# Cross-attention's last step: weight splits, norms, token halves and statistics put behind the chain of the last quarter

## The reference

```python
x = layernorm(x + self_attention(x))                 # 32 heads of 16, causal
x = layernorm(x + cross_attention(x, ctx, ctx, mask))  # 32 query heads of 128, 8 key/value heads
x = layernorm(x + moe(x))                            # top 4 of 16 experts, and a shared expert

# cross_attention
q, k, v = x @ wq, ctx @ wk, ctx @ wv                 # wq 512x4096, wk and wv 512x1024
q, k = rope(q), rope(k)
w = softmax(where(mask, q @ k.T / sqrt(128), -1e9))  # a group of 4 query heads shares a key head
out = (w @ v) @ wo                                   # wo 4096x512
```

## Time and profile before

| | |
|---|---|
| median of three runs | 1835.05 us |
| profiled execution | 1827.3 us, its span 1825.5 us |
| busy share of the span | TensorE 94%, VectorE 73%, ScalarE 50%, GpSimd 49% |
| end of the cross-attention block | 1324.2 us after the span's start |
| what comes after it | routing and shared expert, then 79 expert tiles, then the last layer norm |

### The profile page before, as it was taken

One profiled execution on the slowest core, in us unless ns is written; L12 is line 12 of the kernel. 1 busy time (PEld: TensorE's weight loads), 2 busy tenths in 40 slices (PEclk: granted clock), 3 DMA queues, 4 the chain that ended last, 5 costly groups with the idle time before them and its releaser, 6 DMA issues. The chain is left out here.

```text
span 1825.5 us, 39028 instructions
## 1 busy us (share of the span) xinstructions
PE 1717.9 (94%) x15412; PEld 992.6 (54%) x15412; DVE 1337.6 (73%) x2260; ACT 917.5 (50%) x1532; POOL 894.6 (49%) x732
## 2 busy tenths in 40 slices
PE   6999999899999999999999999999798999999990
PEld 4767666455555555555555555555454555455550
DVE  5788788688888888888888888887788444344445
ACT  4565656655546555555555554646531333233334
POOL 6643022554646555555546464646342555455540
PEclk9999999999999999999999999999899999999995
DMA  9620010211413213223222131212135678887658
GB/s 250 170 47 21 8 61 3 93 65 41 139 58 100 85 61 112 69 73 113 70 70 93 36 123 40 93 47 71 64 123 176 151 151 219 208 215 152 118 97 288
DMA packets 84947, 190.41 MB, mean 104 GB/s; under 512 B 10849, under 2 KB 29665, under 8 KB 82721
## 3 DMA queue, kind: packets, MB, share of 16 engines
q1 hardware_dynamic: 61680, 129.55, 21.0%
q0 software_dynamic: 23088, 58.37, 15.7%
HBM read 124.68 MB, written 63.21 MB: 103 GB/s over the span
## 5 line engine op out<-in xcount | busy, mean ns | idle before, releaser
L288 PE MATMUL bank<-xhl,front_h 128*128 128x512 f16 x704 | 267.8, 380 | 15.0 <-DVEq L68 13.4
L289 PE MATMUL bank<-xhl,front_h 128*128 128x512 f16 x704 | 267.6, 380 | 0.0
L290 PE MATMUL bank<-xhl,front_l 128*128 128x512 f16 x704 | 267.6, 380 | 0.0
L1000 POOL TENSOR_TENSOR xa_xs<-xa_xs,sn 128x512 f32<-128x512 f32 x160 | 233.7, 1460 | 45.8 <-ACT xa_xs L1047 45.8
L1011 POOL TENSOR_TENSOR xa_sc<-xa_sc,xa_rs 128x1024 f32<-128x1024 f32 x32 | 62.2, 1945 | 382.3 <-DVE xa_rs L1241 382.3
L1005 POOL TENSOR_TENSOR xa_rr<-xa_x,xa_xs 128x512 f32<-128x512 f32 x160 | 231.7, 1448 | 12.7 <-DVE xa_x L1147 0.2
L288 PE MATMUL bank<-out_h,xa_oh 128*128 128x512 f16 x512 | 194.1, 379 | 9.3 <-DVE xa_ol L1132 6.6
L1880 POOL DMA_INDIRECT scratch_y<-raw_front,moe_to x79 | 125.2, 1585 | 150.3 <-DVE mo_zl L1933 112.6
L290 PE MATMUL bank<-out_h,xa_ol 128*128 128x512 f16 x512 | 194.0, 379 | 0.0
L289 PE MATMUL bank<-out_l,xa_oh 128*128 128x512 f16 x512 | 194.0, 379 | 0.0
L1046 ACT ACTIVATE xa_xs<-bank 64x512 f32<-64x512 f32 x160 | 94.9, 593 | 131.7 <-PE bank L290 128.0
(11 more groups left out here) (292 smaller groups left out, 4758.1 us busy)
## 6 DMA issues: line engine op xcount, KB each, us to landing
xa_rawc<-in_ew SPq DMA_DIRECT2D x32, 768.0 KB, 5.6
moe_ring<-scratch_w SPq DMA_DIRECT2D x16, 1536.0 KB, 8.7
scratch_w<-xa_chunk_h SPq DMA_DIRECT2D x32, 384.0 KB, 2.3
scratch_w<-xa_chunk_l SPq DMA_DIRECT2D x32, 384.0 KB, 3.3
raw_front<-in_xwq SPq DMA_DIRECT2D x8, 1024.0 KB, 7.8
raw_out<-in_xwo SPq DMA_DIRECT2D x8, 1024.0 KB, 5.3
scratch_y<-xa_zero SPq DMA_DIRECT2D x18, 256.0 KB, 6.0
acc<-in_x POOLq DMA_DIRECT2D x4, 1024.0 KB, 12.8
```

The source lines that it names most:

```text
L288: pe.matmul(out_ap, ah, bh, start=start and m == 0, stop=False)
L289: pe.matmul(out_ap, ah, bl, start=False, stop=False)
L290: mm = pe.matmul(out_ap, al, bh, start=False, stop=stop and m == n - 1)
L1000: PO.mark(pool.tensor_tensor(xr, xr, sn[:, :].rearrange("p (a s) -> p a s", a=1) .to_broadcast([P, QT // S, S]), ALU.mult), f"sm{r}", st)
```

## The change

Everything stands in the last step (7, 3) and the tail. In the step, the high half of the last weight chunk is no longer made behind the exponentials, nor its low half at the step's end. The low half of the shared expert's weights is no longer made between `w0` and `w1`. Of the low token halves of quarter 0, two stay where they were and two move behind the reciprocal. In the tail, the statistics of quarter 2 move from first place on VectorE to behind the `back_lo` splits; the chunk's high half follows `back_p` on ScalarE, its low half follows the statistics and the aggregation on VectorE, and the shared expert's low half stands between the inverse and the adds of `w1` to `w3`. Two semaphores replace the events for the last chunk; the events' counts are kept by naming them with others.

```diff
@@ SyncE, in the loop over steps
-                            sp.wait_ge(DV.sem, DV.value("cl", Step(i, q)))
-                            met(sp)
+                            if (i, q) == (NG - 1, NQ - 1):
+                                sp.wait_ge(s_last_l, 1)
+                            else:
+                                sp.wait_ge(DV.sem, DV.value("cl", Step(i, q)))
+                                met(sp)
                             store_chunk(i, q)
@@ ScalarE, step
+                    def chunk_hi(i, q):
+                        act.wait_ge(s_cr, i * (16 * NQ) + 16 * (q + 1))
+                        act.wait_ge(s_cw, i * (32 * NQ) + 32 * (q + 1))
+                        return act.activation(chunk_h[:, :], rawc[:, :], ACT.Copy, scale=WS)
...
-                        act.wait_ge(s_cr, i * (16 * NQ) + 16 * (q + 1))
-                        act.wait_ge(s_cw, i * (32 * NQ) + 32 * (q + 1))
-                        AC.mark(act.activation(chunk_h[:, :], rawc[:, :], ACT.Copy, scale=WS), "ch", st)
+                        if (i, q) != (NG - 1, NQ - 1):
+                            AC.mark(chunk_hi(i, q), "ch", st)
@@ ScalarE, tail
                     back_p(Step(None, 0))
+                    chunk_hi(NG - 1, NQ - 1).then_inc(s_last_h, 1)
                     back_o(Step(None, 0), range(4))
@@ VectorE, step
-                            back_add(st, [0])
-                        if q == 3:
+                            back_add(st, [0], ("wfl",) if (i, q) == (NG - 1, NQ - 1) else ())
+                        if q == 3 and i < NG - 1:
                             dve.wait_ge(AC.sem, AC.value("wfh", st))
                             DV.mark(split_front_lo(dve, i), "wfl", st)
...
-                        if i == NG - 1 and q == 3:
-                            for t in range(TQ):
+                        last = (i, q) == (NG - 1, NQ - 1)
+                        if last:
+                            for t in range(2):
                                 after.low(dve, 0, t, bank[4 + t])
...
                         DV.mark(dve.reciprocal(rs[:, :, :], sm[:, :, :]), "rc", st, ("w3",) if alone else ())
+                        if last:
+                            for t in range(2, TQ):
+                                after.low(dve, 0, t, bank[4 + t])
                         if not alone:
-                            back_add(st, [3])
-                        dve.wait_ge(AC.sem, AC.value("ch", st))
-                        DV.mark(dve.scalar_tensor_tensor(chunk_l[:, :], ...), "cl", st)
+                            back_add(st, [3], ("cl",) if last else ())
+                        if not last:
+                            dve.wait_ge(AC.sem, AC.value("ch", st))
+                            DV.mark(chunk_lo(), "cl", st)
@@ VectorE, tail
-                    dve.wait_ge(DV.sem, DV.value("w3", st, 1))
-                    after.statistics(dve, 2, range(TQ))
                     back_p_lo(st)
                     for t in range(TQ):
                         after.low(dve, 1, t, bank[(2, 3, 0, 1)[t]])
+                    back_lo(st, range(4))
+                    dve.wait_ge(DV.sem, DV.value("w3", st, 1))
+                    after.statistics(dve, 2, range(TQ))
                     after.aggregate(dve, 2)
-                    back_lo(st, range(4))
+                    dve.wait_ge(s_last_h, 1)
+                    chunk_lo().then_inc(s_last_l, 1)
                     dve.wait_ge(s_gate, 16)
...
                     back_add(st, [0])
                     after.inverse(dve, 2, 1)
+                    dve.wait_ge(AC.sem, AC.value("wfh", Step(NG - 1, NQ - 1)))
+                    split_front_lo(dve, NG - 1)
                     back_add(st, [1, 2, 3])
```

More of the change, by code:

```diff
@@ L864, in cross_attention @@
                 s_cr, s_cw, s_xr = sem("xa_s_cr"), sem("xa_s_cw"), sem("xa_s_xr")
+                s_last_h, s_last_l = sem("xa_last_h"), sem("xa_last_l")
                 zero, s_zero, s_zeros = b("zero", [P, D]), sem("xa_zero"), sem("xa_zeros")
@@ L1098, in step @@
                             s2 = sc[:, h, :, :, :].rearrange("p a b c -> p (a b c)")
-                            AC.mark(act.activation(s2, s2, ACT.Exp, scale=float(HD2) ** -0.5), f"ex{h}", st)
-                        act.wait_ge(s_cr, i * (16 * NQ) + 16 * (q + 1))
-                        act.wait_ge(s_cw, i * (32 * NQ) + 32 * (q + 1))
-                        AC.mark(act.activation(chunk_h[:, :], rawc[:, :], ACT.Copy, scale=WS), "ch", st)
+                            AC.mark(act.activation(s2, s2, ACT.Exp, scale=float(HD2) ** -0.5), f"ex{h}", st,
+                                    ("ch",) if (i, q, h) == (NG - 1, NQ - 1, 1) else ())
+                        if (i, q) != (NG - 1, NQ - 1):
+                            AC.mark(chunk_hi(i, q), "ch", st)
                         if i == NG - 1 and q >= 2:
@@ L1133, in back_lo, with chunk_lo, back_add @@
                                                       heads(oh, tp, b2), ALU.subtract), f"lo{c}", st)
-                    def back_add(st, ts=range(TQ)):
+                    def chunk_lo():
+                        return dve.scalar_tensor_tensor(chunk_l[:, :], rawc[:, :], WS, chunk_h[:, :], ALU.mult, ALU.subtract)
+                    def back_add(st, ts=range(TQ), also=()):
                         for t in ts:
@@ L1139, in back_add @@
                             DV.mark(dve.scalar_tensor_tensor(row, home[f"w{t}"][:, :], 1 / (WS * OS), row,
-                                                             ALU.mult, ALU.add), f"w{t}", st)
+                                                             ALU.mult, ALU.add), f"w{t}", st, also)
                     def cosine(st, r, also=()):
@@ L1241, in step @@
                         DV.mark(dve.reciprocal(rs[:, :, :], sm[:, :, :]), "rc", st, ("w3",) if alone else ())
+                        if last:
+                            for t in range(2, TQ):
+                                after.low(dve, 0, t, bank[4 + t])
                         if not alone:
-                            back_add(st, [3])
-                        dve.wait_ge(AC.sem, AC.value("ch", st))
-                        DV.mark(dve.scalar_tensor_tensor(chunk_l[:, :], rawc[:, :], WS, chunk_h[:, :], ALU.mult, ALU.subtract), "cl", st)
+                            back_add(st, [3], ("cl",) if last else ())
+                        if not last:
+                            dve.wait_ge(AC.sem, AC.value("ch", st))
+                            DV.mark(chunk_lo(), "cl", st)
                     for i in range(NG):
@@ L2133, in build @@
             ln2 = NormSteps("ln2", numbered("st", 0) + ["ag0", "iv0", "sh0"] + numbered("st", 1) + ["ag1", "iv1", "sh1"] + numbered("lo", 0)
-                            + numbered("st", 2) + numbered("lo", 1) + ["ag2", "iv2", "sh2"] + numbered("st", 3) + ["ag3", "lo2.0", "iv3", "sh3"]
+                            + numbered("lo", 1) + numbered("st", 2) + ["ag2", "iv2", "sh2"] + numbered("st", 3) + ["ag3", "lo2.0", "iv3", "sh3"]
                             + numbered("lo", 2, (1, 2, 3)) + numbered("lo", 3),
```

## The result

The changed kernel takes 1833.93 us (median of 20 runs, 1830.23 to 1838.46), the kernel before 1828.87 us (median of 20, 1825.58 to 1836.12). The ratio is 1.0027, 95% interval 1.0018 to 1.0036: 3.3 to 6.6 us slower, a quarter of a per cent. TensorE reached the tail's output matmuls 8 us sooner, and yet the barrier behind them came 5.4 us later.

The account below looks back on a forecast made before the run. TensorE was taken to set the barrier at 1324.2 us, SyncE 0.9 behind; the chunk's 6.9 us delay through SyncE's chain puts it at 1330.1, +5.9 us: 1833.2 profiled, 1841 on the median, 1838 taken; range 1828 to 1845.

Parts of the forecast that it names:

- the two levels of three runs: Runs before: one at 1825.58 us, two near 1835.5; the new median was put between the levels, at 1838.
- The gain ahead of it: Last step and tail's front: reciprocal ready at 1294.9 us, output matmuls starting at 1304 instead of 1311.62, 7.6 us earlier.
- The chunk's low half: VectorE's tail: the last chunk's low half, taking 3.13 us, ends at 1311.0 instead of 1304.09, 6.9 us later.
- SyncE's chain: Chunk store, quarter 0 rows, GpSimd's quarter 1 pass, second store: 18.9 us without slack, all moved on by 6.9 us.
- The new idle of 3.4 us: TensorE's tail output matmuls: wait for VectorE's add of w0 to free bank 0 before w2, 3.4 us.
- Behind the barrier: Next block, entered with TensorE idle for 7 to 10 us: 0 cost, 1.5 us as upper bound.
- the idle start: TensorE enters the block behind the barrier from idle instead of full clock; taken as 0, at most 1.5 us.
- Rival 1: At the barrier: TensorE sets the end after all, 0.9 to 3.5 us earlier, 1823.8 to 1826.4 us profiled; 10%.
- Rival 2: Shared expert's matmuls behind the barrier: TensorE stays at 1.2 GHz, +22 us with the shift, 1849 us profiled; 4%.
- Rival 3: At the barrier: little of the chunk's 6.9 us delay arrives, 0 to +4 us, 1827 to 1831 us profiled; 12%.

Follow-up runs that it names:

- experiment 1: The changed kernel with SyncE storing both sets of token rows ahead of the last weight chunk; ratio 0.9971 to the kernel before.
- experiment 3: The changed kernel with only the last chunk's split put back into the step; ratio 0.9977 to the kernel before.
- experiment 4: The changed kernel with the last chunk's low half moved to the very end of VectorE's tail; ratio 1.0075 to the kernel before.
- experiment 5: The kernel before with only the last chunk's high and low halves moved as in the change; ratio 1.0051 to the kernel before.
- experiment 2: The kernel before with both sets of token rows stored ahead of the last weight chunk; ratio 1.0013 to the kernel before.
- experiment 6: The changed kernel with 52 unused matmuls added at the end of TensorE's tail; ratio 1.0030 to the kernel before.
- experiment 7: As experiment 1, with the adds of w0 and w1 moved earlier in VectorE's tail, w0's ahead of the chunk's low half; ratio 0.9953 to the kernel before.

## Why the prediction was right

The forecast was +5.9 us against the profiled execution of before, through one mechanism: the last chunk's store comes later, the rows stand behind it in SyncE's queue, GpSimd behind the rows, their store behind GpSimd. Measured were +5.4 us to the barrier and +5.1 us between the medians. Experiments 1, 3, 4 and 5 show the mechanism from four sides, and experiment 2 that TensorE, not this chain, set the barrier before. 1838 us as the median was 4 us high: I had put it between the two levels of three runs, and with 20 runs the median of before is 1828.87, not 1835.05.

**The gain ahead of it.** Reciprocal forecast at 1294.9, measured 1294.7 on before's time; output matmuls at 1304, measured 1303.4. Up to here the sum was right almost to the row (the product's end, 1294.9 + 1.90, is 1296.8 and not 1296.9; nothing hangs on it).

**The chunk's low half** was the mis-sized term: forecast to end at 1311.0, it ended at 1308.9 on before's time, 4.8 us later than before and not 6.9. I took its 3.13 us from the earlier trace rows; it took 1.73, which is 1.4 us of the 2.1, and the rest is that VectorE reached it 0.7 us sooner., read beside it, tells why. GpSimd's product ran until 1300.58 + 1.90 = 1302.48, and the low half started at 1300.96: 1.52 us of its 3.13 lie beside the product, and 1.61 remain. In experiment 3, where the product ends 0.33 us into it, it took 1.94. In experiment 2 the roles are reversed, as the timelines of GpSimd and VectorE show:

```profile
1302.98 2.14 POOL L244 CAST raw_out<-acc 128x512 f16<-128x512 f32 x1
```

```profile
1301.52 3.13 DVE L1249 SCALAR_TENSOR_TENSOR xa_chunk_l<-xa_rawc,xa_chunk_h 128x1536 f16<-128x1536 f32 x1
```

A copy of 0.61 us took 2.14: 1.67 us until VectorE's split ended at 1304.65, and 0.47 behind it. In experiment 3 the copy of 2.75 us is made up in the same way, of the 2.28 us of the split beside it and 0.47. The Trainium skill, SBUF — State Buffer, section Who interferes with whom, says that a VectorE instruction with two inputs in SBUF contends with a GpSimd instruction that reads SBUF, over a port pair that is an exclusive lock, and that the order of issue decides who blocks. These rows agree: the split takes 1.73 alone, and 1.61 once the neighbour's part is taken off 3.13.

**SyncE's chain** was taken over as 18.9 us from the low half's end to SyncE's freedom and measured 1328.4 - 1308.11 = 20.3 us. The excess of 1.4 us lies in the store of rows (8.45 us from the low half to GpSimd's start, before 7.04). From SyncE's freedom to the barrier it was 0.4 us (1328.4 to 1328.78), where the forecast had 0.2 as an estimate. So the barrier's 1330.1 of the forecast was 1329.6 on before's time: 2.1 us less for the low half, 1.4 more for the store, 0.2 more at the barrier. That two of the errors nearly cancel is luck; the path was right, and its terms were off by more than the sum.

**The new idle of 3.4 us** on TensorE for the add of `w0` did not come. The low half ended earlier, the gate's split took 0.4 us instead of about 1, and some of the first output matmuls ran at the slow clock (0.67 on average in 1304 to 1308 us), so that `w0` had been added (at 1309.07) before `w1` ended: the stretch from 1302.58 to 1314.82 took 12.2 us instead of 10.4, with a stop of 0.2 us ahead of `w3`. In experiment 1 the clock stood high and the idle came, 1.30 us. TensorE ended at 1316.73, 1317.5 on before's time, ahead of the 1320.4 to 1323.0 of the forecast. That miss did not reach the time, as TensorE had 12 us to spare.

**Behind the barrier** I had taken 0 with 1.5 us as the upper bound; measured were 1.5 us in the one trace, at that bound. The reason I gave for the bound, the idle start, is refuted by experiments 1, 4 and 6. With it the trace is 6.9 us longer up to the list, a little more than the interval of the total allows (3.3 to 6.6), so not every execution of the change need have the 1.5 us.

**The rivals.** Rival 1 (TensorE sets the end) is what experiment 1 makes true. There the barrier came 6.4 us earlier than before, where the rival had 0.9 to 3.5: its price was reckoned with the idle of 3.4 us and the slow clock behind it. Rival 2 (TensorE enters the shared expert's matmuls at the low clock and stays there) did not happen: the clock was low only for the first 3.6 us of these matmuls, and 1.00 from 1348 on. Rival 3 (0 to +4) didn't either, though one of its grounds did hold in part: VectorE reached the chunk earlier than summed.

## What to carry to other kernels

Before a piece of work is put off into idle time, follow its product and not its engine: which DMA waits for it, what stands behind that DMA in the same queue, and who waits for that. When an engine's idle row names a DMA whose source had been ready long before, look at what is ahead of it in the queue; issuing it first made the same change a gain. And a duration read from a trace belongs to its neighbours: the 3.13 us of a VectorE split held 1.52 us of blocking by GpSimd.

## What was not expected of the hardware

The store of rows landed about 1.4 us later in the traces in which a packet of the instruction queue (`q8`) fell into the stretch of the stores. The DMA view of the stretch of the stores, of the change, with KB and us to landing:

```profile
q8 instruction: 1, 0.02, 0.6%
issues: line engine op xcount, KB each, median us to landing
scratch_x<-raw_out SPq DMA_DIRECT2D x1, 512.0 KB, 5.5
scratch_x<-raw_front SPq DMA_DIRECT2D x1, 512.0 KB, 7.0
```

The same view of experiment 4, which has no `q8` line:

```profile
scratch_x<-raw_out SPq DMA_DIRECT2D x1, 512.0 KB, 4.2
scratch_x<-raw_front SPq DMA_DIRECT2D x1, 512.0 KB, 5.4
```

In the changed kernel the rate falls from 343 to 33 GB/s at 1314 and trickles on at about 20 until 1316, with a busy share of 0.06 over the 16 DMA engines, as if one of them still had its share to do. The same is seen in experiments 5 and 6 (one such packet, 6.8 and 7.0 us), and not in the traces of before and of experiments 3 and 4 (none, 5.4 to 5.5 us). These six traces agree. In experiments 1, 2 and 7, where the rows of quarter 0 are stored with nothing ahead of them, such a packet is there too and the store landed in 4.6 us, only 0.4 more than the 4.2 of the second set in the traces of before and of the change, which have none there. No experiment moved the packet alone, so this is a correlation.

The expert tiles, whose code is the same in all kernels, took 387.4 to 392.3 us in the nine profiled executions, from the first matmul on their weights to the first store of the output. The profiled execution of the change had the longest of these (before: 387.8), which is 4.5 of the 10.5 us by which it differs from that of before. That one pair of executions shows twice the loss of the medians (5.1).
